# Normalised rows kept as split halves, and transposes, routing and a wait moved to other rounds of an attention and expert kernel

## What is computed

```python
xn = layernorm(x)                                   # no scale, no bias, eps 1e-5
# attention: 16 heads of 128, 4 key/value heads, each for 4 query heads
q, k, v = xn @ Wq, xn @ Wk, xn @ Wv
q, k = rope(q) * xscale, rope(k) / xscale
s = softmax(causal(q @ k.T / sqrt(128))) @ v  @ Wo
# experts: 16 of width 176, top 2 by softmax of the router, and a shared one of width 352
scores = softmax(xn @ gate_w.T); topk_w, topk_idx = top_k(scores, 2)
y = sum_e combine_e * (silu(g_e) * u_e) @ w_down_e  + swiglu(xn @ shared_gate_up) @ shared_down
out = x + s * silu(y)
```

## Time and profile before

| | |
|---|---|
| median of 3 runs | 716.62 us (714.23 to 716.69) |
| profiled execution | 723.3 us, span 721.5 us, mean granted clock of TensorE 0.984 |
| busy share | PE 90%, DVE 81%, POOL 75%, ScalarE 61% |
| prologue, to the first copy of V | 42.9 us |
| rounds, from the first copy of V in round 0 to that in round 15 | 486.9 us |
| from there to the end | 191.8 us |

### The profile page before, as it was taken

One profiled execution on the slowest core, in us unless ns is written; L12 is line 12 of the kernel. 1 busy time (PEld: TensorE's weight loads), 2 busy tenths in 40 slices (PEclk: granted clock), 3 DMA queues, 4 the chain that ended last, 5 costly groups with the idle time before them and its releaser, 6 DMA issues.

```text
span 721.5 us, 16449 instructions
## 1 busy us (share of the span) xinstructions
PE 651.3 (90%) x4930; PEld 456.4 (63%) x4996; DVE 580.8 (81%) x1684; ACT 441.6 (61%) x1206; POOL 537.6 (75%) x586
## 2 busy tenths in 40 slices
PE   2668999999999989999999999999989999999982
PEld 1245667666666757666666666666667777677651
DVE  6987999999999998899999989899974553333378
ACT  3576766675565656676676667667686845554542
POOL 4576878779788979899988989999898935444500
PEclk9999999999999999999999999999999999999995
DMA  9583000004100000000000000000054615555672
GB/s 305 176 252 102 2 1 3 1 1 120 33 1 1 8 18 15 22 15 15 15 15 22 15 22 15 15 15 17 2 93 148 184 23 137 131 133 140 212 263 102
DMA packets 65104, 50.61 MB, mean 70 GB/s; under 512 B 35392, under 2 KB 58400, under 8 KB 65056
## 3 DMA queue, kind: packets, MB, share of 16 engines
q1 hardware_dynamic: 60944, 39.45, 19.4%
q0 software_dynamic: 3840, 10.52, 4.6%
q10 hardware_dynamic: 272, 0.02, 0.0%
HBM read 24.73 MB, written 18.96 MB: 61 GB/s over the span
## 4 chain that ended last, share of the span: by engine, by line
PE 27%; POOL 26%; DVE 23%; issue 15%; ACT 7%; DMA 2%; POOLq 0%; SPq 0%; DVEq 0%
POOL arena L557 11%; PE bank L1594 9%; POOL arena L544 6%; PE bank L1624 6%; POOL arena L551 4%; DVE arena L1128 4%; ACT arena L780 4%; DVE arena L1103 3%; DVE arena L1102 3%; PE bank L1438 2%; POOL compare L586 2%; POOL xs_dram L590 2%; PE bank L1467 2%; PE bank L1451 2%; PE bank L1603 2%
## 5 line engine op out<-in xcount | busy, mean ns | idle before, releaser
L557 POOL TENSOR_TENSOR arena<-arena,rinv 128x128 f32<-128x128 f32 (+3 forms) x256 | 176.2, 718 | 51.2 <-DVE rinv L1122 50.8
L780 ACT ACTIVATE arena<-bank,nmax 128x512 f32<-128x512 f32 (+3 forms) x256 | 132.5, 534 | 53.8 <-DVE nmax L1116 53.7
L1116 DVE CUSTOM_DVE_ANT_0 bank<-bank,mask_b 128x512 f32<-128x512 f32 (+3 forms) x256 | 118.0, 517 | 7.0 <-issue 6.9
L1407 PE MATMUL bank<-xnT_hi,arena 128*128 128x512 f16 (+1 forms) x320 | 110.2, 386 | 12.4 <-DVE arena L1103 7.6
L788 ACT CAST arena<-bank 128x512 f16<-128x512 f32 (+1 forms) x192 | 94.0, 526 | 43.9 <-PE bank L1451 42.9
L1438 PE MATMUL bank<-arena 128*128 128x384 f16 (+7 forms) x736 | 113.4, 296 | 3.2 <-POOL arena L551 1.3
L1467 PE MATMUL bank<-arena 128*128 128x512 bf16 (+2 forms) x765 | 115.9, 301 | 0.2
L1128 DVE TENSOR_TENSOR arena<-bank,arena 128x512 bf16<-128x512 f32 (+1 forms) x192 | 108.9, 595 | 4.2 <-ACT arena L788 3.1
L1451 PE MATMUL bank<-ident_f,arena 128*128 128x128 f32 x640 | 93.2, 276 | 13.3 <-DVE arena L1128 8.3
L544 POOL TENSOR_TENSOR arena<-arena 128x512 f32<-128x512 f32 x77 | 98.6, 1281 | 3.0 <-DVE arena L1103 3.0
L551 POOL TENSOR_TENSOR arena<-arena 128x512 bf16<-128x512 f32 x80 | 92.3, 1161 | 4.7 <-ACT arena L768 4.7
(11 more groups left out here) (146 smaller groups left out, 1172.8 us busy)
## 6 DMA issues: line engine op xcount, KB each, us to landing
xs_dram<-s_sb SPq DMA_DIRECT2D x4, 1548.0 KB, 14.6
stage<-w_gate_up SPq DMA_DIRECT2D x16, 352.0 KB
arena<-ys_dram SPq DMA_DIRECT2D x8, 512.0 KB, 8.3
stage<-w_down SPq DMA_DIRECT2D x16, 176.0 KB
stage<-wq SPq DMA_DIRECT2D x4, 512.0 KB, 8.6
stage<-wo SPq DMA_DIRECT2D x4, 512.0 KB, 6.1
stage<-x SPq DMA_DIRECT2D x1, 2048.0 KB
out<-s_sb SPq DMA_DIRECT2D x8, 256.0 KB, 2.1
```

Source lines behind the costliest of these rows:

```text
L557: ins = pool.tensor_tensor(pr, pr, rinv[:, par, qt:qt + 1].to_broadcast([P, (qt + 1) * P]), ALU.mult)
L780: ins = act.activation(probs[par][:, P_AT[qt]:P_AT[qt] + n], score_bank[u][:, col:col + n], ACT.Exp, scale=-1.0, bias=nmax[:, par, qt:qt + ...
L1116: ins = dve.tensor_tensor_reduce(score_bank[u][:, col:col + n], score_bank[u][:, col:col + n], mask_b[:, S - n:S], -1.0, 3e38, ALU.add, AL ...
L1407: ins = pe.matmul(ps[:], w[a][:, c * chunk:c * chunk + DH], tokens[m][:, c * TOK:c * TOK + S], start=(c == 0 and n == 0), stop=(c == KC - ...
```

## The change

1. x is loaded into `s_sb` and normalised in place (`xn_t` is now a view of it). The normalised rows are kept in a new `row_sb` as high and low halves with four tags: the weights of the first and the second expert, the token's row number, and the number of its second slot plus 1. ScalarE makes the high halves (`split_hi`), POOL the low ones (`split_lo`), and POOL then clears the batch's part of `s_sb` (`clear_sum`) for the sum of the projections. A row of `xs_dram` grows from 258 to 260 columns.
2. The inverse root is POOL's power instead of ScalarE's Sqrt. POOL's first weight differences wait for the normalisation; chunk 3's goes from DVE to POOL; k is projected first, then q0. The statistics of batches 1 to 3 go to round 0 (DVE), their roots and shifts to round 1 (POOL, `refine_roots`). The fill and the last two weight chunks change places on SP.
3. The fill's source is now in the part of `arena` where `oT` lies, so ScalarE waits for the fill (`fill_out`) ahead of the first `output_hi` in round 0.
4. The transposes of batches 1 to 3 are made from the halves, 4 in float16 and 4 in bfloat16 an item, in rounds 2, 3 and 4, two items a round. ScalarE copies both halves out of PSUM. It adds to nothing: the item's place in `misc_free` is given by DVE with the first product of the next rope, which waits for the copies. ScalarE also normalises batch 1 in round 1, and batches 2 and 3 in rounds 2 and 3, half a batch behind each item.
5. Routers: batch 0 in round 1, batch 1 in round 3, batches 2 and 3 in round 4. All routing steps come later (rounds 5 to 8). Of the tile numbers the comparison is one operation on POOL, and the sum and the group numbers 15 small matmuls.
6. Scatter: the DMAs read `row_sb` as it is. `set_out` and `rows_low` are gone. The scatter runs in rounds 8 (4 DMAs), 9 to 12 (6 each) and 13 (4). POOL's rounds are all written out.
7. Which of the two weights a routed row takes is worked out by POOL in round 15 from the tags (`read_tags`).

The core of the diff:

```diff
-ITEMS_FIRST = ["q0", "v", "x10", "q1", "x11", "x20", "k", "x21", "x30", "q2", "q3", "x31"]
-ITEMS_LOGITS = ["q0", "v", "g0", "q1", "o0", "g1", "k", "o1", "g2", "q2", "o2", "q3", "o3", "g3"]
+ITEMS_FIRST = ["q0", "v", "q1", "k", "q2", "q3"]
+ITEMS_G0 = ["q0", "v", "g0", "q1", "o0", "k", "o1", "q2", "o2", "q3", "o3"]
+ITEMS_X1 = ["q0", "v", "q1", "o0", "x10", "k", "o1", "x11", "q2", "o2", "q3", "o3"]
...
-            pool.memset(s_sb[:], 0.0).then_inc(zeroed, 1)
+            pool.memset(fill, 0.0).then_inc(zeroed, 1)
...
+            pool.wait_ge(var_ready, 1)
+            pool.tensor_tensor(rstd[:, token_tiles(0)], var[:, token_tiles(0)], power[:, token_tiles(0)], ALU.pow).then_inc(rooted, 1)
+            pool.wait_ge(xn_first, QT)
+            for n in range(W_EARLY):
                 weights_lo(n)
...
-            def rows_low(t):
-                token = xn[:, bass.ds(t * D, D)].rearrange("p (o d) -> p o d", o=1).to_broadcast([P, TOP_K, D])
-                pool.tensor_tensor(rows_lo, token, rows_hi, ALU.subtract).then_inc(rows_split, 1)
...
+            def split_lo(b):
+                hi, lo = row_halves(token_tiles(b))
+                pool.wait_ge(rows_hi, b + 1)
+                pool.tensor_tensor(lo, xn_t[:, token_tiles(b), :], hi, ALU.subtract).then_inc(rows_lo, 1)
...
+            def scatter(t, n):
+                pool.indirect_dma_start(xs_dram, bass.IndirectOffsetOnAxis(slot_u[:, bass.ds(t * TOP_K + n, 1)], 0),
+                                        row_sb[:, bass.ds(t * DX, DX)], None).then_inc(scattered, 16)
...
+            def x_item_in(rd, c):
+                b = X_BATCH[rd.early]
+                name = f"x{b}{c}"
+                at = c * TOK + b * S
+                ps = misc_bank[rd.bank(name)][:]
                 act.wait_ge(misc_ps, rd.item(name))
+                act.copy(xnT[0][:, at:at + S], ps.bitcast(F16)[:, 0:S])
+                act.copy(xnT[1][:, at:at + S], ps.bitcast(BF16)[:, S:2 * S]).then_inc(xnT_in, 1)
...
+                    if rd.first and j == 2:
+                        act.wait_ge(fill_out, 16 * FILLS)
                     if j == 2:
                         output_hi(rd, 0)
...
+                    if rd.early in X_BATCH and j > 0:
+                        x_item_in(rd, j - 1)
+                    if rd.early in (2, 3) and j > 0:
+                        normalise(rd.early, j - 1)
...
+                if copied_x is not None:
+                    dve.wait_ge(xnT_in, copied_x)
+                ins = dve.tensor_tensor(rot_a[buf], ps[:], tab[:, cos, :], ALU.mult)
+                if copied_x is not None:
+                    ins.then_inc(misc_free, 1)
...
-            with pool.Fori(LOOP_FROM, LATE) as i:
-                round_(Round(i, "pair"))
+            for n in range(1, LATE):
+                round_(Round(n))
```

More of the change, by code:

```diff
@@ L464, in _ @@
                 sp.dma_start(xs_tiles[:, c * FILL_TILES:(c + 1) * FILL_TILES], fill).then_inc(fill_out, 16)
+            for n in range(N_CHUNKS - 2, N_CHUNKS):
+                load_weights(n)
             sp.wait_ge(w_lo, N_CHUNKS)
@@ L696, in round_ @@
                         expert_lo(j)
-                    if rd.first and j == 2:
-                        pool.wait_ge(fill_out, 16 * FILLS)
-                        pool.memset(fill[:, :, D + 1], 0.0).then_inc(zeroed, 1)
                 if not rd.last:
@@ L707, in _ @@
             round_(Round(0, "first"))
-            for n in range(1, LOOP_FROM):
-                round_(Round(n, "pair" if n == SCATTER_FROM else "loop"))
-            with pool.Fori(LOOP_FROM, LATE) as i:
-                round_(Round(i, "pair"))
+            for n in range(1, LATE):
+                round_(Round(n))
             round_(Round(LATE, "late"))
@@ L1269, in _ @@
             for n in range(1, LOOP_FROM):
-                round_(Round(n, "pair" if n == SCATTER_FROM else "loop"))
-            with dve.Fori(LOOP_FROM, LATE) as i:
-                round_(Round(i, "pair"))
+                round_(Round(n))
+            with dve.Fori(LOOP_FROM, LOOP_TO) as i:
+                round_(Round(i))
+            round_(Round(LOOP_TO))
             round_(Round(LATE, "late"))
@@ L1547, in _ @@
                 pe.wait_ge(w_lo, WEIGHTS_BY[n])
-                round_(Round(n, "pair" if n == SCATTER_FROM else "loop"))
-            with pe.Fori(LOOP_FROM, LATE) as i:
-                round_(Round(i, "pair"))
+                if n == NKV - 1:
+                    pe.wait_ge(xnT_in, KC)
+                if n == 2 * NKV - 1:
+                    pe.wait_ge(xnT_in, KC * (B - 1))
+                round_(Round(n))
+            with pe.Fori(LOOP_FROM, LOOP_TO) as i:
+                round_(Round(i))
+            round_(Round(LOOP_TO))
             round_(Round(LATE, "late"))
```

466 lines of the change are left out of this document (252 added, 214 removed).

## The result

The changed kernel takes 740.46 us (739.32 to 742.41, five runs), the kernel before 716.62 (714.23 to 718.32); the ratio is 1.0337, 95% interval 1.0316 to 1.0359. On another occasion, on one chip, it was 740.23 against 715.75, ratio 1.0346 (1.0315 to 1.0377). I had said 728.4, with a range up to 738: slower was right, but only half of the size was forecast.

The account below looks back on a forecast made before the run. PE was taken as the floor of a round at about 30.7 us, with DVE nearly as full. Terms -1.9 - 3.5 + 23.9 - 6.7 = +11.8 us, set on the median 716.62, gave 728.4 us, range 708 to 738.

Parts of the forecast that it names:

- The term for the prologue and round 0: Start through round 0: 5.9 us saved in the prologue, 4.0 eaten by ScalarE waiting for the fill, -1.9 us net.
- round 1 was -3.5: Round 1: three of four routers leave, at 1.16 us each, so it falls from 35.33 to 31.84 us.
- rounds 5 to 13 were -6.7: Rounds 5 to 13: later routing steps, a cheaper round 8 and less POOL work in scatter rounds give -6.7 us.
- The two waits: Rounds 2 to 4: PE idles ahead of o1 and o2 until DVE's rope product, 3.35 and 2.85 us in rounds 2, 3.
- the stall of the first normalisations: Prologue: DVE's four first normalisations took 5.02 us beside POOL's weight differences; with POOL waiting, 1.4, so 3.6 saved.
- the extra stall on the first sum: Prologue: POOL's later weight differences might stall DVE's first sums of k and q0; 1.4 us, turning -1.9 into -0.5.
- the fill's wait: Round 0: ScalarE waits 4.0 us for the fill of xs_dram ahead of its first attention output copy.
- the other end: Round 1: POOL's power at 2.13 us instead of 0.20, which would give back about 1.5 us of the gain.
- PE is next late at 31.0: Rounds 9 to 13: POOL falls to 29.3 us a round, so PE bounds them at 31.0 against 31.7; -3.4 us.
- The first, that ScalarE's queue doesn't matter: Rounds 2 to 4: ScalarE's copies overlap DVE's work, only the late bank release costs, +9.1; total 713.6 us; chance 0.16.
- The faster case: As the first rival, with the fill out before ScalarE asks, so all 5.9 us come through; total 709.6 us; chance 0.17.
- The clock's case: PE's clock falls at all six waits of rounds 2 to 4 and behind the fill; +20.3, total 736.9 us; chance 0.20.

Follow-up runs that it names:

- the release: Changed kernel, but in rounds 2 to 4 output projections o1 and o2 wait for ScalarE's x item copies, not DVE's next rope product: 730.16 us, ratio 1.0121.
- on the queue: Changed kernel, but in rounds 2 to 4 ScalarE copies x items behind the attention output and normalises half a batch later in the round: 729.29 us, ratio 1.0112.
- on both: Changed kernel with o1 and o2 waiting for ScalarE's x item copies, and these copies made behind the attention output: 719.49 us, ratio 1.0056 to the kernel before.
- the one in the kernel of before: Kernel before, with three idle ScalarE copies added ahead of each of two attention outputs in rounds 2 to 4: 727.4 against 720.41 us, ratio 1.0107.
- the branch: Changed kernel with rounds 9 to 12 written out on PE, ScalarE and DVE too, so without loop turns there: 739.98 us.

## Why the prediction was wrong

Part by part, with the kernel of before in its second profile and the changed one in its second, since these have no stall in the prologue:

| | before | after | difference | forecast |
|---|---|---|---|---|
| to the first copy of V | 41.21 | 36.95 | -4.3 | -5.9 |
| round 0 | 38.63 | 44.97 | +6.3 | +4.0 |
| round 1 | 35.33 | 33.64 | -1.7 | -3.5 |
| rounds 2 to 4 | 94.16 | 119.48 | +25.3 | +23.9 |
| rounds 5 to 8 | 130.09 | 128.16 | -1.9 | -3.3 |
| rounds 9 to 13 | 158.60 | 156.38 | -2.2 | -3.4 |
| round 14 | 30.57 | 30.78 | +0.2 | 0 |
| sum | | | +21.8 | +11.8 |

So the sum failed in its sizes, all on the same side. The term for the prologue and round 0 was -1.9 and measured +2.1; round 1 was -3.5 and measured -1.7; rounds 2 to 4 were +23.9 and measured +25.3; rounds 5 to 13 were -6.7 and measured -4.1. The first of these is the largest, 4.0 of the 10 us.

**Rounds 2 to 4 were right.** The two waits were forecast as 3.35 and 2.85 us and are 3.21 and 2.74, in round 4 2.3 and 1.8 against 2.24 and 1.77. Round by round 39.4, 40.6, 38.0 were said, and 40.0, 41.8 and 38.8 are in the first profile, 40.0, 40.6 and 38.8 in the second, which had just the two falls of the clock that were counted. What is over in the table is thus 0.6 in round 2 and 0.8 in round 4; in the first profile the clock was low for 3.4 us more. The experiments on the release, on the queue and on both, and the one in the kernel of before, show both halves of the mechanism.

**The prologue was taken from one execution.** The 3.6 us for the stall of the first normalisations were in that profile and not in the next, so the gain is 4.3 in the table. Against the first profile it is 5.9, as forecast, but that is luck. The stall of 3.6 was worth 1.65 at the first copy of V, since without it DVE still had to wait for x and to finish the statistics of the later batches before the first rope product. This product came 2.0 us earlier, not 3.6 (the first profile of before, then the second):

```profile
19.63 0.69 DVE L1098 TENSOR_TENSOR arena<-bank,tab 128x512 f32<-128x512 f32 x1
```

```profile
16.63 0.91 DVE L972 BATCH_NORM_AGGREGATE mv<-stats 128x2 f32<-128x6 f32 x12
17.57 0.17 DVE L974 TENSOR_SCALAR var<-mv 128x12 f32<-128x12 f32 x1
17.65 0.69 DVE L1098 TENSOR_TENSOR arena<-bank,tab 128x512 f32<-128x512 f32 x1
```

The power cost 0.8 in the prologue, by the variant with the multiplication. And the extra stall on the first sum, which I had priced at 1.4 against the change, is not there. On the contrary, the first of these sums took 2.10 us in both profiles of before and takes 0.69 in the changed kernel, where POOL's differences of weights are over by 17.2:

```profile
10.89 6.29 POOL L554 TENSOR_TENSOR arena<-stage,arena 128x1024 bf16<-128x1024 f32 x3 [2.29 <-DVE s_sb L1072]
```

```profile
18.77 0.69 DVE L1210 TENSOR_TENSOR arena<-arena 128x512 f32<-128x512 f32 x1
```

The rule that I cited stands for the normalisations too: the Trainium skill, "SBUF — State Buffer" (section "Who interferes with whom"), says that issue order decides who is blocked. The two executions agree, 5.02 us with POOL 0.03 us ahead and 1.38 with DVE 1.1 us ahead.

**Round 0** missed by 2.3 us (2.4 by the first profiles). I took the fill's wait as what is left when everything moves by 5.9, so 4.0 us, with the copy ready at 50.7, the fill out at 54.7 and 24.7 us from there to round 1. The copy was ready at 47.6 (first profile): without the x items round 0 is also faster up to that place, 10.6 us behind the first copy of V instead of 13.7. I had noted that the x items leave a round that waits anyway, and counted nothing for it. The wait is thus 8.5 us. But a copy that is ready earlier only waits longer; it doesn't move what follows. The 2.4 us are these two: the fill, let go 5.9 earlier, was out at 56.1, so it took 1.4 us longer than worked out (two chunks of Wo were now issued behind it, at 45.2; that these slowed it was not tested), and from the copy to round 1 it was 25.8 instead of the 24.7 that I took from before, which was not taken apart. The variant without the wait shows the gain that was eaten: round 0 at 35.8, 2.8 less than before the change.

**Round 1** missed by 1.8: POOL's power takes 2.30 us. I had given this as the other end, with a loss of 1.5, and took the small end because the operation has few columns. With the multiplication round 1 is 31.70, against a forecast of 31.84.

**Rounds 5 to 13** missed by 2.6 together. I had read PE's floor as 30.7 from round 2, the shortest window of the table. The plain rounds are 30.7 (round 2 before, round 5 after) or 31.4 (round 5 before, round 7 after), and with scatters 31.5 after the change, though POOL waits for others there. So the step "PE is next late at 31.0" was 0.5 too low for rounds 10 to 12, though right within 0.3 for rounds 9 and 13 (30.7 and 31.1). In rounds 5 to 8 what is over is round 8: 33.5 us against 31.8, with PE waiting 1.05 us for DVE ahead of the tile matmuls and 0.5 for POOL ahead of scores; the others together came out as forecast to 0.2.

**The rivals.** The first, that ScalarE's queue doesn't matter, would have been 713.6; it is refuted by the run of the kernel of before with idle copies, and by the runs with ScalarE's order changed, alone and on top of the release. The faster case is refuted too: the fill was not out. The clock's case (736.9) was nearest to the time but for another reason: of its six falls two or three happened in each profile. My range ended at 738, just above this highest of the rivals, each of which moves one or two terms; here all terms missed on the same side.

**What stays open.** The profiles account for 22 us; 24 are measured. Which wait brings a fall of the clock is not settled. Why the fill took 1.4 us longer, and the stretch behind it 1.0 more, is open. What holds rounds 10 to 12 at 31.5 with PE busy for 30.9 was not taken further than that it is not the branch, and that POOL has idle time in them.

## What to carry to other kernels

Before work is put into an engine's queue, look at what stands behind it there and who waits for that: 1 to 2 us of copies and scaling ahead of one small copy cost some 3.2 us at each of six places together with a bank released late, and 0.9 without the late release, while the same work behind the copy, with the bank released in time, was nearly free. Let a buffer be released by whoever read it last, not by a later instruction of a third engine that happens to come in the right order. And look at a second profile of the kernel before when a term of the sum rests on a stall at its start.
